# Half fills of two banks for the scores of the second layer's first pass, and a new order of steps

## The chip, the cores and the metric

The kernel runs on one core of a Trainium2 chip. The metric is the device time of one execution in microseconds (us). Times of single instructions come from one profiled execution.

## What is computed

Two transformer blocks on x of 8 images (batch entries) of 512 tokens of 256 numbers. The first block has linear and windowed attention and a gated feed; the second, which the change touches, is:

```python
x1, x2 = jnp.split(x, 2, axis=-1)                 # rotation of queries and keys
attn = jnp.einsum('bqhd,bkhd->bhqk', Q, K) * scale     # 16 heads of 16 numbers
attn = jnp.where(causal, attn, NEG_INF)
attn = jax.nn.softmax(attn, axis=-1)
out = jnp.einsum('bhqk,bkhd->bqhd', attn, V).reshape(B, S, dim)
x = x + ga * (out @ w_proj + b_proj)
h = silu(tlin(h, w1)) * tlin(h, w2)               # 256 -> 1024
h = gelu(tlin(h, h1)); h = gelu(tlin(h, h2))      # 1024 -> 1024, twice
x = x + gb * tlin(h, w3)
```

## The kernel before

The kernel is a list of steps, `ORDER`, written out as text. An entry `1:max.0.2.1` is layer 1 (the second), step `max`, image 0, group of heads 2, fill 1. Every engine walks the whole list and runs its own part of each step, so each engine works strictly in the list's order and waits on semaphores for the others.

PSUM has 8 banks. They are dealt out as named rooms: `wide` is banks 0 to 3, `low` banks 0 and 1, `high` banks 2 and 3, `acc` bank 4, `misc` bank 5, `f0` and `f1` banks 6 and 7. Each room has a semaphore for filled and one for freed, counted by `fills_of`, which also finds for each fill who used its banks last. `slot_of` names the room of a step of the second layer.

The attention of an image goes over four groups of four heads. Scores are computed twice. For the row maxima, steps `max` with j = 0, 1, 2 (L1952) write query blocks of 128 against all keys up to them: j = 0 has 512 keys, j = 1 has 384 and 128 keys, j = 2 has 256. A product takes 32 rows of the array; the four heads of a group stand on its four strips of 32 rows and in the four banks of `wide`. VectorE masks the diagonal block of the four heads (L1686) and reduces them to maxima (L1689); after j = 2 it writes the shift columns (L1697, L1698). Step `again` turns these (L1938, and L1742 on VectorE). Then steps `att` with j = 0, 1, 2 write shift plus scores with keys on the partitions (L1964, L1968), ScalarE takes the exponential of four heads at once (L1843) into one of two buffers `probs`, GpSimd zeroes what lies above the diagonal (L1608), and TensorE multiplies with the values (`values`, L1984). ScalarE releases the room only when its result is written (L1846). Steps `tq` and `tk` bring queries and keys of a group (L1931; L1832, L1835 on ScalarE, L1736 on VectorE), `heads` and `turn` carry the result back (L1993, L2002; L1749, L1751).

The second layer's first pass overlaps the first layer's last steps: `r`, `kk` and `last` (L1120, L1130 on TensorE; the mixes L742 and L745, and L752, L755, L757 on VectorE), `out` (L1108), the flag (L597 to L600, L1152). Later passes overlap with the feed of the image before them: `up` (L2025), `h1` and `h2` (L2041). `norm` normalises (L1649), `stats` is L1640 and L1643, `proj` is L1922 with the rotation on VectorE (L1666 to L1679).

Of the kernel before, what the change touches and what calls it, by code (L numbers as in the profile page):

```python
# [1227 lines left out]
0:lv.14.2 0:lin.15.1 0:wv.14.1 0:lv.15.0 0:lh.14 0:fold.16 0:pair.16 0:v.4.1 0:tq.17 0:wv.15.0 0:win.15.1 0:turn.3.2 0:again.16 0:wt.13.0 0:wt.13.1
0:lin.16.0 0:wh.14 0:tk.17 0:stats.5 0:lv.15.1 0:lv.15.2 0:wv.15.1 0:win.16.0 0:lh.15 0:lv.16.0 0:wh.15 0:fold.17 0:lin.16.1 0:turn.3.3 0:tq.18
0:turn.3.1 0:wm.17.0 0:out.3.0 0:pair.17 0:tk.18 0:out.3.1 0:lin.17.0 0:lv.16.1 0:lv.16.2 0:wt.14.0 0:wv.16.0 0:win.16.1 0:lin.17.1 0:tq.19 0:xT.3.0  # L1230
0:wv.16.1 0:wm.18.0 0:again.17 0:fold.18 0:lv.17.0 0:tk.19 0:xg.4 0:pair.18 0:lh.16 0:lv.17.1 0:xT.3.1 0:lin.18.0 0:again.18 0:fold.19 0:win.17.0
# [955 lines left out]
```

## Time and profile before

| | us |
|---|---|
| median of 3 runs | 1977.19 |
| lowest, highest | 1975.2, 1977.64 |
| profiled execution | 1979.78 |
| its span | 1978.0 |

The span is that of the trace. Times in rows count from its start. A granted clock (PEclk) of 1.00 is TensorE at 2.4 GHz, its other level is 1.2 GHz, and a mean between is time spent at both. PE is TensorE, PEld its weight loads, DVE VectorE, ACT ScalarE, POOL GpSimd. A name with q (ACTq) is the engine's queue of semaphore instructions. A wait for several semaphores is put down to the one that came last.

### The profile page before, as it was taken

The page shows a single profiled execution, that of the slowest core. Times are in us where ns is not written, and L with a number is a line of the kernel's source. Part 1 is how long each engine was busy: PE and PEld are TensorE (multiplying, and loading weights), DVE is VectorE, ACT ScalarE, POOL GpSimd, SP SyncE. Part 2 cuts the span into 40 slices and gives each one's busy share as a digit, 9 for nine tenths or more (in the row PEclk, how much of TensorE's full clock was granted, in tenths as well). Part 3 has the DMA queues.
Part 4 walks back from the last instruction along what each step waited for, and adds up shares of the span by engine and source line. Part 5 has one row for each costly group of instructions (what it writes and reads, how often), then busy time and mean ns, then how long its engine had stood idle before and what let it go on. Part 6 is the DMA issues. An engine that isn't in the chain of part 4 may idle for free.

```text
span 1978.0 us, 39009 instructions
## 1 busy us (share of the span) xinstructions
PE 1856.4 (94%) x15449; PEld 1293.8 (65%) x15449; DVE 1375.4 (70%) x2407; ACT 907.2 (46%) x1116; POOL 510.0 (26%) x597
## 2 busy tenths in 40 slices
PE   7998999899999998887999999999999999999998
PEld 4665657565666664444677676676776776776787
DVE  5667677766776677778768678587588678587443
ACT  2656574656565653332444524524534434534431
POOL 2434353443444342121211203102204003112120
PEclk8898999999999999888999999999999999999999
DMA  6221213221321110400122122221231231221321
GB/s 184 58 46 42 59 37 73 50 58 28 86 52 26 40 39 5 171 1 17 44 81 78 54 85 62 65 87 50 75 96 30 86 93 44 86 84 43 112 83 43
DMA packets 171812, 126.26 MB, mean 64 GB/s; under 512 B 113944, under 2 KB 148720, under 8 KB 171248
## 3 DMA queue, kind: packets, MB, share of 16 engines
q1 hardware_dynamic: 170800, 123.74, 22.6%
q8 instruction: 127, 2.08, 0.4%
q14 instruction: 53, 0.43, 0.1%
q10 hardware_dynamic: 832, 0.01, 0.0%
HBM read 103.66 MB, written 20.03 MB: 63 GB/s over the span
## 4 chain that ended last, share of the span: by engine, by line
PE 77%; DVE 15%; ACT 4%; issue 3%; POOL 1%; DMA 0%; SPq 0%; DVEq 0%; POOLq 0%; ACTq 0%
PE ps L2041 24%; PE ps L2025 5%; PE ps L1078 5%; PE ps L1922 4%; PE ps L1984 3%; PE ps L983 3%; PE ps L1952 3%; PE ps L2055 2%; PE ps L1108 2%; PE ps L1041 2%; PE ps L1130 2%; PE ps L1023 2%; DVE b_maxima L1689 2%; PE ps L1968 2%; PE ps L1964 2%
## 5 line engine op out<-in xcount | busy, mean ns | idle before, releaser
L2041 PE MATMUL ps<-b_acts,b_hidden_w 128*128 128x512 f32 x2048 | 504.6, 398 | 1.1 <-POOL b_acts L1616 1.1
L2041 PEld LDWEIGHTS ps<-b_acts,b_hidden_w 128*128 128x128 f32 x2048 | 376.2, 188 | 90.9 <-issue 9.8
L452 POOL TENSOR_SCALAR_AFFINE_SELECT a_probs<-a_probs 128x512 f32<-128x512 f32 (+1 forms) x224 | 166.3, 758 | 357.4 <-ACT a_probs L863 249.1
L1608 POOL TENSOR_SCALAR_AFFINE_SELECT b_work<-b_work 128x512 f32<-128x512 f32 x128 | 83.3, 663 | 673.1 <-ACT b_work L1843 673.0
L1879 ACT ACTIVATE b_acts_exact<-ps,c_s 128x512 f32<-128x512 f32 x128 | 88.2, 689 | 297.6 <-PE ps L2041 297.4
L863 ACT ACTIVATE a_probs<-ps 128x2048 f32<-128x2048 f32 (+1 forms) x96 | 153.2, 1595 | 123.5 <-DVEq L713 86.7
L1843 ACT ACTIVATE b_work<-ps 128x2048 f32<-128x2048 f32 (+1 forms) x96 | 153.4, 1597 | 90.8 <-PE ps L1968 89.0
L1689 DVE TENSOR_REDUCE b_maxima<-ps 128x4 f32<-128x2048 f32 (+3 forms) x128 | 187.9, 1489 | 3.3
L1787 DVE CAST b_acts<-b_acts_exact 128x512 fp32r<-128x512 f32 x128 | 55.8, 436 | 164.2 <-ACT b_acts_exact L1879 163.9
L1078 PE MATMUL ps<-a_probs,c_va 128*17 128x192 f32 (+4 forms) x2048 | 136.6, 388 | 2.9 <-issue 1.5
L1686 DVE TENSOR_TENSOR ps<-ps,c_causalr 128x512 f32<-128x512 f32 x128 | 86.1, 696 | 45.2 <-PE ps L1952 43.4
L1616 POOL TENSOR_TENSOR b_acts<-b_acts_exact,b_acts 128x512 fp32r<-128x512 f32 x64 | 82.5, 1289 | 134.0 <-DVE b_acts L1780 112.8
L1952 PE MATMUL ps<-c_k_split,c_q_split 32*128 32x512 f32 (+3 forms) x1024 | 68.5, 363 | 29.6 <-DVE b_maxima L1689 13.8
L1788 DVE TENSOR_TENSOR b_acts<-b_acts_exact,b_acts 128x512 fp32r<-128x512 f32 x128 | 88.7, 693 | 4.4
L1984 PE MATMUL ps<-b_work,c_va 128*17 128x512 f32 (+3 forms) x1024 | 88.4, 451 | 2.2 <-POOL b_work L1608 1.7
L1078 PEld LDWEIGHTS ps<-a_probs,c_va 128*17 128x17 f32 x2048 | 48.0, 98 | 58.9 <-issue 40.1
L1922 PE MATMUL ps<-c_wqkv,b_work 128*128 128x512 f32 (+1 forms) x256 | 85.6, 486 | 0.0
L1871 ACT ACTIVATE b_acts_exact<-ps,c_s 128x512 f32<-128x512 f32 x64 | 44.1, 689 | 89.1 <-PE ps L2025 87.6
L1952 PEld LDWEIGHTS ps<-c_k_split,c_q_split 32*128 32x128 f32 x1024 | 42.2, 192 | 63.7 <-issue 23.9
L2025 PE MATMUL ps<-b_acts,b_w2T 128*128 128x512 f32 x256 | 77.6, 426 | 0.9 <-DVEq L1795 0.6
L457 POOL TENSOR_SCALAR_AFFINE_SELECT a_probs<-a_probs 128x1024 f32<-128x1024 f32 (+2 forms) x96 | 74.7, 794 | 4.4
L2025 PE MATMUL ps<-b_acts,b_w1T 128*128 128x512 f32 x256 | 75.6, 419 | 0.3 <-issue 0.3
(244 smaller groups left out, 3577.4 us busy)
## 6 DMA issues: line engine op xcount, KB each, us to landing
b_hidden_w<-turned_h SPq DMA_DIRECT2D x128, 512.0 KB, 3.5
a_raw_next<-in_L_ffn_h_w SPq DMA_DIRECT2D x512, 16.0 KB, 1.8
turned_h<-a_staged SPq DMA_DIRECT2D x32, 256.0 KB, 2.1
a_x<-in_L_attn_x SPq DMA_DIRECT2D x8, 512.0 KB, 4.6
x_mid<-a_x SPq DMA_DIRECT2D x16, 256.0 KB, 2.2
c_x<-x_mid SPq DMA_DIRECT2D x8, 512.0 KB, 3.9
out<-c_x SPq DMA_DIRECT2D x16, 256.0 KB, 2.5
turned_w<-a_staged SPq DMA_DIRECT2D x12, 256.0 KB, 2.4
```

The source lines that it names most:

```text
L452: return nc.gpsimd.affine_select(out=z, in_=z, compare_op=ALU.is_ge, fill=0.0, base=0, pattern=[[0, blocks_n], [1, cols]], channel_multipl ...
L863: nc.scalar.activation(pb, here[:, :, o:o + w], ACT.Square, bias=1.0, scale=0.5).then_inc(att_ready, 1)
L1078: ins = nc.tensor.matmul(here[R * i:R * i + HD + 1, kb * P:kb * P + q], va[:, b % 2, kb, 4 * g + i, :], pb[:, first + i * pitch:first + i ...
L1689: ins = nc.vector.tensor_reduce(maxima[:, t, :].unsqueeze(2), room["wide"][:, :, o:o + (t + 1) * P], AX.X, ALU.max, negate=True)
L1788: nc.vector.tensor_tensor(dst[:, 1], z, dst[:, 0].bitcast(F32), ALU.subtract).then_inc(h_split, 1)
L1843: ins = nc.scalar.activation(probs[nth % 2][:, 0:4 * w].rearrange("p (h q) -> p h q", q=w), here[:, :, 0:w], ACT.Exp, scale=float(HD) ** -0.5)
L1879: nc.scalar.activation((exact_a if name == "h2" else exact_b)[:, m], here, ACT.Gelu, scale=s12[:, 2 + (name == "h2"), m:m + 1]).then_inc(g ...
L1922: ins = nc.tensor.matmul(here[:, a, 0:w], hT[:, k, t * P:(t + 1) * P], wqkv[:, k, o:o + w], start=(k == 0), stop=(k == ND - 1))
L1952: ins = nc.tensor.matmul(here[:, i, o:o + (t + 1) * P], part[rows_of(i), g % 2, t * P:(t + 1) * P], ksplit[rows_of(i), g % 2, 0:(t + 1) * ...
L1984: ins = nc.tensor.matmul(room["acc"][R * i:R * i + HD + 1, kb * P:S], va[:, kb, 4 * g + i, :], probs[nth % 2][:, i * w + o:i * w + o + S - ...
L2025: ins = nc.tensor.matmul(here, view((w1T, w2T)[j][:, i, k]), view(h2r[:, k, part]), start=(k + part == 0), stop=(k == ND - 1 and part == 1))
L2041: ins = nc.tensor.matmul(here, view(hidden_w[:, m, k]), view(src[:, k, i]), start=(k + i == 0), stop=(k == NHID - 1 and i == 1))
```

## The change

Only image 0 of the second layer is split. There each `max` becomes two steps `maxh` and each `att` two steps `atth`, with a last number 0 or 1: heads 0 and 1 of the group in room `low`, heads 2 and 3 in room `high`. Each half has its own filled and freed counts. Products, masked squares and maxima are the same in sum; each VectorE and ScalarE instruction there handles two heads instead of four, so there are twice as many. GpSimd's zeroing stays whole and runs after the second half. The order of steps is another one from image 4 of the first layer on to the last pass; most steps of the second layer's later passes keep their place within a few.

Line numbers in the changed kernel are higher: its masks are L1714, maxima L1717, score fills L1998, weight fills L2011 and L2015, the normalisation L1654.

VectorE, ahead of the passage: normalisation of the second layer's image 0 and the first layer's mixes. Before:

```order
L742 TENSOR_SCALAR a_mix<-a_xT,a_one_mu 128x512 x2
L745 SCALAR_TENSOR_TENSOR a_mix<-a_xT,a_mu,a_mix 128x512 [waits a_dve_own_result]
L745 SCALAR_TENSOR_TENSOR a_mix<-a_xT,a_mu,a_mix 128x512
L1649 TENSOR_SCALAR b_work<-c_x,b_meanvar,b_rstd 128x256 [waits b_rstd0_ready,a_sumsq_ready,a_x_plus_h_ready]
L1649 TENSOR_SCALAR b_work<-c_x,b_meanvar,b_rstd 128x256 x3
L566 RECIPROCAL a_rden<-ps 128x16 [waits m1_free,m0_full]
L568 TENSOR_TENSOR a_onat<-ps,a_rden 128x4x64 [waits a_dve_own_result]
L566 RECIPROCAL a_rden<-ps 128x16 [waits m1_free,m1_full]
L568 TENSOR_TENSOR a_onat<-ps,a_rden 128x4x64 [waits a_dve_own_result]
L755 TENSOR_SCALAR a_oT<-ps 128x512 [waits m0_full]
L757 TENSOR_TENSOR a_oT<-a_oT 128x512 [waits a_dve_own_result]
L1666 TENSOR_TENSOR b_work<-ps,c_cossin 128x512 [waits m0_full,a_staged1_placed,a_staged0_placed,high_full]
```

Now:

```order
L1654 TENSOR_SCALAR b_work<-c_x,b_meanvar,b_rstd 128x256 [waits b_rstd0_ready,a_sumsq_ready,a_x_plus_h_ready]
L1654 TENSOR_SCALAR b_work<-c_x,b_meanvar,b_rstd 128x256 x3
L742 TENSOR_SCALAR a_mix<-a_xT,a_one_mu 128x512 [waits a_xT_half_ready]
L742 TENSOR_SCALAR a_mix<-a_xT,a_one_mu 128x512
L745 SCALAR_TENSOR_TENSOR a_mix<-a_xT,a_mu,a_mix 128x512 [waits a_dve_own_result]
L745 SCALAR_TENSOR_TENSOR a_mix<-a_xT,a_mu,a_mix 128x512
L742 TENSOR_SCALAR a_mix<-a_xT,a_one_mu 128x512 x2
L745 SCALAR_TENSOR_TENSOR a_mix<-a_xT,a_mu,a_mix 128x512 [waits a_dve_own_result]
L745 SCALAR_TENSOR_TENSOR a_mix<-a_xT,a_mu,a_mix 128x512
L1645 BN_STATS b_stats<-c_x 128x6 x4
L1648 BN_AGGR b_meanvar<-b_stats 128x2 [waits b_dve_own_result]
L1648 BN_AGGR b_meanvar<-b_stats 128x2 x3
```

The mixes, and the statistics of image 2, stand behind the normalisation now, where before the mixes stood ahead of it.

VectorE, the first maxima of image 0. Before:

```order
L1686 TENSOR_TENSOR ps<-ps,c_causalr 128x4x128 [waits wide_full]
L1689 TENSOR_REDUCE b_maxima<-ps 128x4 [waits b_dve_own_result]
L1736 TENSOR_TENSOR c_q_split<-ps,c_q_split 128x512 [waits b_high_queries_turned,misc_full]
L1686 TENSOR_TENSOR ps<-ps,c_causalr 128x4x128 [waits wide_full]
L1686 TENSOR_TENSOR ps<-ps,c_causalr 128x4x128
L1689 TENSOR_REDUCE b_maxima<-ps 128x4 [waits b_dve_own_result]
L1689 TENSOR_REDUCE b_maxima<-ps 128x4
L752 SCALAR_TENSOR_TENSOR a_oT<-a_oT,a_gb 128x512 [waits a_feed_gate_ready,a_tanh_r_ready]
```

Now:

```order
L1714 TENSOR_TENSOR ps<-ps,c_causalr 128x2x128 [waits low_full]
L1717 TENSOR_REDUCE b_maxima<-ps 128x2 [waits b_dve_own_result]
L1714 TENSOR_TENSOR ps<-ps,c_causalr 128x2x128 [waits high_full]
L1717 TENSOR_REDUCE b_maxima<-ps 128x2 [waits b_dve_own_result]
L1714 TENSOR_TENSOR ps<-ps,c_causalr 128x2x128 [waits low_full]
L1714 TENSOR_TENSOR ps<-ps,c_causalr 128x2x128
L1717 TENSOR_REDUCE b_maxima<-ps 128x2 [waits b_dve_own_result]
L1717 TENSOR_REDUCE b_maxima<-ps 128x2
```

The waits for `wide` have become waits for `low` and `high` by turns, and the queries' second part (L1736) and L752 have moved out from between.

TensorE, where weight fills and score fills follow each other. Before, groups 1 and 2:

```order
L1964 MATMUL ps<-c_k_split,c_shift_rows 128x384 [waits wide_free]
L1964 MATMUL ps<-c_k_split,c_shift_rows 128x384 x3
L1968 MATMUL ps<-c_q_split,c_k_split 128x384 x8
L1964 MATMUL ps<-c_k_split,c_shift_rows 128x128 x4
L1968 MATMUL ps<-c_q_split,c_k_split 128x128 x8
L1952 MATMUL ps<-c_k_split,c_q_split 128x512 [waits misc_free,wide_free]
L1952 MATMUL ps<-c_k_split,c_q_split 128x512 x7
```

Now, groups 0 and 1:

```order
L2011 MATMUL ps<-c_k_split,c_shift_rows 128x512 [waits misc_free,low_free]
L2011 MATMUL ps<-c_k_split,c_shift_rows 128x512
L2015 MATMUL ps<-c_q_split,c_k_split 128x512 x4
L1088 MATMUL ps<-c_identr,a_sums 128x128 [waits acc0_free,m0_free]
L1088 MATMUL ps<-c_identr,a_sums 128x128 x3
L2011 MATMUL ps<-c_k_split,c_shift_rows 128x512 [waits misc_free,high_free]
L2011 MATMUL ps<-c_k_split,c_shift_rows 128x512
L2015 MATMUL ps<-c_q_split,c_k_split 128x512 x4
L1998 MATMUL ps<-c_k_split,c_q_split 128x384 [waits low_free]
L1998 MATMUL ps<-c_k_split,c_q_split 128x384 x3
```

A score fill that waited for the whole room now waits for one half, with the other half's weight fill ahead of it.

The diff; of the table one line before and one after are shown:

```diff
-0:lh.30 0:lin.31.2 1:max.0.0.0 1:tk.0.1 1:tq.0.1 0:lv.31.0 1:max.0.0.1 0:r.6.0 1:max.0.0.2 1:max.0.1.0 1:again.0.0 0:r.6.1 1:max.0.1.1 0:last.6.0
...
+0:lh.30 0:lin.31.0 0:r.6.1 1:tq.0.0 0:lin.31.1 0:kk.6.1 1:tk.0.0 0:lin.31.2 0:wh.31 1:tq.0.1 1:maxh.0.0.0.0 1:tk.0.1 1:maxh.0.0.0.1 1:maxh.0.0.1.0
...
@@ -1335,6 +1338,8 @@
     name = step[0]
     if name in ("max", "att"):
         return "wide"
+    if name in ("maxh", "atth"):
+        return ("low", "high")[step[4]]
     if name in ("hT", "xT"):
         return "low"
     if name == "proj":
@@ -1589,7 +1594,7 @@
             name, b = step[:2]
             if name == "stats":
                 power(0, b)
-            elif step == ("max", 0, 0, 2):
+            elif step == ("maxh", 0, 0, 2, 0):
                 nc.gpsimd.memset(shift_cols[:], 0.0).then_inc(shift_zero, 1)
             elif name == "ga":
 
@@ -1597,8 +1602,8 @@
                 pool.wait_ge(ga_ready, 32 * (b + 1))
                 xb = x[:, b % 3]
                 nc.gpsimd.tensor_tensor(xb, xb, ga[:, 1:2, :].broadcast_to([P, NT, D]), ALU.add).then_inc(xg_ready, 1)
-            elif name == "att":
-                g, j = step[2:]
+            elif name == "att" or name == "atth" and step[4]:
+                g, j = step[2:4]
                 nth = (b * QUADS + g) * 3 + j
                 pool.wait_ge(att_ready, nth + 1)
                 w = ATT_WIDTH[j]
@@ -1697,6 +1702,29 @@
             link(nc.vector.tensor_copy(shift_high.bitcast(F32R), maxima[:]))
             nc.vector.tensor_tensor(shift_low.bitcast(F32R), maxima[:], shift_high, ALU.subtract).then_inc(shift_ready, 1)
 
+        def half_maximum(step):
+
+            b, g, j, pair = step[1:]
+            free = arrive(step)
+            here, heads = room[slot_of(step)], slice(2 * pair, 2 * pair + 2)
+            if j + pair == 0 and g:
+                dve.wait_ge(shift_ready, b * QUADS + g)
+            for t, o in MAX_FILLS[j]:
+                square = here[:, :, o + t * P:o + (t + 1) * P]
+                ins = nc.vector.tensor_tensor(square, square, causal[:, None, :].broadcast_to([P, 2, P]), ALU.add)
+            link(ins)
+            for t, o in MAX_FILLS[j]:
+                ins = nc.vector.tensor_reduce(maxima[:, t, heads].unsqueeze(2), here[:, :, o:o + (t + 1) * P], AX.X, ALU.max, negate=True)
+            if j < 2 or pair == 0:
+                ins.then_inc(free, 1)
+                return
+            link(ins)
+            dve.sem_inc(free, 1)
+            if b + g == 0:
+                dve.wait_ge(shift_zero, 1)
+            link(nc.vector.tensor_copy(shift_high.bitcast(F32R), maxima[:]))
+            nc.vector.tensor_tensor(shift_low.bitcast(F32R), maxima[:], shift_high, ALU.subtract).then_inc(shift_ready, 1)
+
         def gated(step, gate, dst, ready):
 
             free = arrive(step)
@@ -1736,6 +1764,8 @@
                 nc.vector.tensor_tensor(qlow[:, nth % 2], room[slot_of(step)], qhigh[:, nth % 2].bitcast(F32), ALU.subtract).then_inc(free, 1)
             elif name == "max":
                 maximum(*step[1:])
+            elif name == "maxh":
+                half_maximum(step)
             elif name == "again":
                 free = arrive(step)
                 by_tile = room[slot_of(step)].rearrange("p (t q) -> p t q", q=P)
@@ -1844,6 +1874,21 @@
                 ins.then_inc(att_ready, 1)
                 act.wait_ge(att_ready, nth + 1)
                 act.sem_inc(free, 1)
+            elif name == "atth":
+                here, free = arrive(step)
+                g, j, pair = step[2:]
+                nth = (b * QUADS + g) * 3 + j
+                w = ATT_WIDTH[j]
+                if nth >= 2:
+                    act.wait_ge(pv_done, nth - 1)
+                heads = probs[nth % 2][:, 0:4 * w].rearrange("p (h q) -> p h q", q=w)[:, 2 * pair:2 * pair + 2]
+                ins = nc.scalar.activation(heads, here[:, :, 0:w], ACT.Exp, scale=float(HD) ** -0.5)
+                if pair:
+                    ins.then_inc(att_ready, 1)
+                    act.wait_ge(att_ready, nth + 1)
+                    act.sem_inc(free, 1)
+                else:
+                    ins.then_inc(free, 1)
             elif name == "values" and step[3] == 2:
                 u = fills["values", b, step[2], 0]
                 act.wait_ge(pv_done, 3 * (b * QUADS + step[2] + 1))
@@ -1940,7 +1985,8 @@
                 ins.then_inc(full_sem, 1)
 
             def max_fill(step):
-                b, g, j = step[1:]
+                b, g, j = step[1:4]
+                heads = range(4) if len(step) == 4 else range(2 * step[4], 2 * step[4] + 2)
                 here, full_sem = take(step)
                 if j == 0:
                     for name in ("tq", "tk"):
@@ -1948,24 +1994,25 @@
                         pe.wait_ge(freed[u.slot], u.free)
                 for t, o in MAX_FILLS[j]:
                     for part in (qhigh, qlow):
-                        for i in range(4):
-                            ins = nc.tensor.matmul(here[:, i, o:o + (t + 1) * P], part[rows_of(i), g % 2, t * P:(t + 1) * P],
+                        for i in heads:
+                            ins = nc.tensor.matmul(here[:, i - heads[0], o:o + (t + 1) * P], part[rows_of(i), g % 2, t * P:(t + 1) * P],
                                                    ksplit[rows_of(i), g % 2, 0:(t + 1) * P], start=(part is qhigh), stop=(part is qlow))
                 ins.then_inc(full_sem, 1)
 
             def scores(step):
-                b, g, j = step[1:]
+                b, g, j = step[1:4]
+                heads = range(4) if len(step) == 4 else range(2 * step[4], 2 * step[4] + 2)
                 here, full_sem = take(step)
                 if j == 0:
                     u = fills["again", b, g]
                     pe.wait_ge(freed[u.slot], u.free)
                 for kb, o in ATT_FILLS[j]:
-                    for i in range(4):
-                        nc.tensor.matmul(here[:, i, o:o + S - kb * P], shift_rows[rows_of(i), NT:NT + 1].broadcast_to([R, P]), shift[rows_of(i), kb * P:S],
+                    for i in heads:
+                        nc.tensor.matmul(here[:, i - heads[0], o:o + S - kb * P], shift_rows[rows_of(i), NT:NT + 1].broadcast_to([R, P]), shift[rows_of(i), kb * P:S],
                                          start=True, stop=False, skip_group_check=True)
                     for part in (qhigh, qlow):
-                        for i in range(4):
-                            ins = nc.tensor.matmul(here[:, i, o:o + S - kb * P], ksplit[rows_of(i), g % 2, kb * P:(kb + 1) * P], part[rows_of(i), g % 2, kb * P:S],
+                        for i in heads:
+                            ins = nc.tensor.matmul(here[:, i - heads[0], o:o + S - kb * P], ksplit[rows_of(i), g % 2, kb * P:(kb + 1) * P], part[rows_of(i), g % 2, kb * P:S],
                                                    start=False, stop=(part is qlow), skip_group_check=True)
                 ins.then_inc(full_sem, 1)
 
@@ -2071,9 +2118,9 @@
                     turn_nat(step)
                 elif name == "again":
                     turn_again(step)
-                elif name == "max":
+                elif name in ("max", "maxh"):
                     max_fill(step)
-                elif name == "att":
+                elif name in ("att", "atth"):
                     scores(step)
                 elif name == "values":
                     values(step)
```

## Rows read from the trace of the kernel before

**Rows 1.** The page, part 1, and part 2's granted TensorE clock in 40 slices.
```profile
PE 1856.4 (94%) x15449; PEld 1293.8 (65%) x15449; DVE 1375.4 (70%) x2407; ACT 907.2 (46%) x1116; POOL 510.0 (26%) x597
...
PEclk8898999999999999888999999999999999999999
```

**Rows 2.** Busy time of each engine by stretches; the columns are in the first line.
```profile
core 0: us, PE busy (x) PEld busy (x) DVE busy (x) ACT busy (x) POOL busy (x), PEclk, DMA share, GB/s
700.00:746.00 46.00, 41.37 (x485) 29.23 (x485) 31.30 (x57) 23.86 (x27) 21.71 (x26) 0.93 0.16 41
746.00:780.80 34.80, 30.16 (x237) 16.43 (x236) 26.82 (x51) 14.75 (x19) 9.80 (x13) 0.95 0.00 1
780.80:867.20 86.40, 66.37 (x605) 39.51 (x604) 62.77 (x100) 29.31 (x29) 12.71 (x19) 0.84 0.26 98
...
960.00:1978.00 1018.00, 994.57 (x6697) 730.77 (x6693) 696.34 (x1177) 415.03 (x473) 170.97 (x183) 0.99 0.25 72
```

**Rows 3.** Waits from 780.7 to 867.2: engine, line, waited for: us, times, longest.
```profile
DVE ps L1686 <- PE ps L1952: 14.9, 9, 4.6
...
PE ps L1964 <- ACTq L1846: 5.0, 5, 2.0
PE ps L1952 <- ACTq L1846: 4.6, 3, 2.0
```

**Rows 4.** Timeline, one turn of a score fill: TensorE, then VectorE.
```profile
820.39 0.74 PE L1952 MATMUL ps<-c_k_split,c_q_split 32*128 32x512 f32 x8 [2.02 <-ACTq L1846]
...
821.92 2.29 DVE L1689 TENSOR_REDUCE b_maxima<-ps 128x4 f32<-128x2048 f32 x1
...
824.27 0.79 PE L1952 MATMUL ps<-c_k_split,c_q_split 32*128 32x384 f32 x16 [0.98 <-DVE b_maxima L1689]
```

**Rows 5.** VectorE's groups, shapes apart, 780.7 to 867.2: count, busy, mean ns.
```profile
L1686 DVE TENSOR_TENSOR ps<-ps,c_causalr 128x512 f32<-128x512 f32 x16 | 10.8, 696 | 14.9 <-PE ps L1952 14.9
L1689 DVE TENSOR_REDUCE b_maxima<-ps 128x4 f32<-128x2048 f32 x4 | 9.2, 2292 | 0.1
L1689 DVE TENSOR_REDUCE b_maxima<-ps 128x4 f32<-128x1536 f32 x4 | 7.0, 1758 | 0.1
L1689 DVE TENSOR_REDUCE b_maxima<-ps 128x4 f32<-128x1024 f32 x4 | 4.9, 1225 | 0.1
...
L1689 DVE TENSOR_REDUCE b_maxima<-ps 128x4 f32<-128x512 f32 x4 | 2.7, 680 | 0.0
...
L1751 DVE TENSOR_TENSOR b_onat<-ps,b_rden 128x256 f32<-128x256 f32 x2 | 0.8, 424 | 0.1
...
L1640 DVE BATCH_NORM_STATS2 b_stats<-c_x 128x6 f32<-128x256 f32 x4 | 1.4, 412 | 0.0
```

**Rows 6.** Timeline of TensorE: a fill for the weights, and one dense product.
```profile
814.29 0.50 PE L1964 MATMUL ps<-c_k_split,c_shift_rows 32*128 32x512 f32 x4
814.63 0.64 PE L1968 MATMUL ps<-c_q_split,c_k_split 32*128 32x512 f32 x8
...
824.99 3.72 PE L1108 MATMUL ps<-a_wout,a_oT 128*128 128x256 f32 x16
```

**Rows 7.** The same stretch for lines L1952, L1964 and L1968 alone, in that order.
```profile
780.80:867.20 86.40, 9.30 (x120) 5.94 (x120) 0.84 0.26 98
...
780.80:867.20 86.40, 6.79 (x64) 3.42 (x64) 0.84 0.26 98
...
780.80:867.20 86.40, 8.18 (x128) 6.31 (x128) 0.84 0.26 98
```

**Rows 8.** ScalarE's smaller exponentials in the same stretch.
```profile
L1843 ACT ACTIVATE b_work<-ps 128x1024 f32<-128x1024 f32 x4 | 4.1, 1024 | 13.7 <-PE ps L1968 13.6
```

**Rows 9.** Timeline of VectorE ahead of the passage.
```profile
746.02 0.88 DVE L742 TENSOR_SCALAR a_mix<-a_xT,a_one_mu 128x512 f32<-128x512 f32 x2 [0.33 <-ACT a_xT L899]
...
751.27 3.40 DVE L1649 TENSOR_SCALAR b_work<-c_x,b_meanvar,b_rstd 128x256 f32<-128x256 f32 x4
...
761.23 0.69 DVE L1666 TENSOR_TENSOR b_work<-ps,c_cossin 128x512 f32<-128x512 f32 x1 [1.05 <-PE ps L1922]
```

More of the change, by code:

```diff
@@ L1228 @@
[L1228 to L1231, printed above, removed]
@@ new lines @@
+1:atth.0.0.0.1 1:maxh.0.1.1.0 1:maxh.0.1.1.1 0:last.6.1 1:atth.0.0.1.0 1:atth.0.0.1.1 1:maxh.0.1.2.0 0:turn.7.0 1:maxh.0.1.2.1 1:values.0.0.0
+1:atth.0.0.2.0 1:atth.0.0.2.1 1:again.0.1 1:values.0.0.1 1:tq.0.2 1:atth.0.1.0.0 0:turn.7.1 1:tk.0.2 1:atth.0.1.0.1 1:maxh.0.2.0.0 0:turn.7.2
+1:maxh.0.2.0.1 0:turn.7.3 1:values.0.0.2 1:maxh.0.2.1.0 1:maxh.0.2.1.1 1:heads.0.0 0:out.7.0 1:atth.0.1.1.0 1:atth.0.1.1.1 1:values.0.1.0
+1:atth.0.1.2.0 1:atth.0.1.2.1 1:tq.0.3 1:maxh.0.2.2.0 1:maxh.0.2.2.1 1:tk.0.3 1:maxh.0.3.0.0 1:maxh.0.3.0.1 1:values.0.1.1 1:maxh.0.3.1.0 1:again.0.2
@@ new lines @@
+1:max.2.0.1 1:tq.2.1 1:h2.0.3.1 1:h2.0.4.0 1:max.2.0.2 1:h2.0.4.1 1:tk.2.1 1:h2.0.5.0 1:heads.1.3 1:max.2.1.0 1:h2.0.5.1 1:h2.0.6.0 1:max.2.1.1
+1:h2.0.6.1 1:turn.1.1 1:h2.0.7.0 1:again.2.0 1:max.2.1.2 1:h2.0.7.1 1:out.1.0 1:att.2.0.0 1:out.1.1 1:last.0.0.0 1:att.2.0.1 1:values.2.0.0
+1:last.0.0.1 1:att.2.0.2 1:values.2.0.1 1:again.2.1 1:xT.1 1:last.0.1.0 1:split.1 1:tq.2.2 1:att.2.1.0 1:last.0.1.1 1:tk.2.2 1:up.1.0.0 1:ga.2
+1:values.2.0.2 1:max.2.2.0 1:up.1.0.1 1:up.1.1.0 1:values.2.1.0 1:heads.2.0 1:att.2.1.1 1:up.1.1.1 1:up.1.2.0 1:att.2.1.2 1:up.1.2.1 1:max.2.2.1
@@ new lines @@
+1:turn.3.1 1:h2.2.7.1 1:att.4.0.0 1:out.3.0 1:out.3.1 1:att.4.0.1 1:values.4.0.0 1:last.2.0.0 1:att.4.0.2 1:tq.4.2 1:last.2.0.1 1:xT.3 1:again.4.1
+1:last.2.1.0 1:tk.4.2 1:split.3 1:values.4.0.1 1:max.4.2.0 1:values.4.0.2 1:last.2.1.1 1:up.3.0.0 1:att.4.1.0 1:heads.4.0 1:up.3.0.1 1:up.3.1.0
+1:att.4.1.1 1:up.3.1.1 1:up.3.2.0 1:max.4.2.1 1:values.4.1.0 1:up.3.2.1 1:values.4.1.1 1:up.3.3.0 1:att.4.1.2 1:max.4.2.2 1:up.3.3.1 1:tk.4.3
+1:up.3.4.0 1:values.4.1.2 1:again.4.2 1:up.3.4.1 1:up.3.5.0 1:heads.4.1 1:att.4.2.0 1:up.3.5.1 1:up.3.6.0 1:tq.4.3 1:att.4.2.1 1:up.3.6.1 1:up.3.7.0
@@ new lines @@
+1:ga.4 1:tk.5.1 1:h2.3.4.0 1:max.5.0.2 1:heads.4.3 1:h2.3.4.1 1:h2.3.5.0 1:again.5.0 1:max.5.1.0 1:h2.3.5.1 1:h2.3.6.0 1:max.5.1.1 1:turn.4.0
+1:h2.3.6.1 1:h2.3.7.0 1:max.5.1.2 1:turn.4.1 1:h2.3.7.1 1:att.5.0.0 1:out.4.0 1:out.4.1 1:att.5.0.1 1:values.5.0.0 1:last.3.0.0 1:att.5.0.2 1:tq.5.2
+1:last.3.0.1 1:xT.4 1:again.5.1 1:last.3.1.0 1:tk.5.2 1:values.5.0.1 1:ga.5 1:split.4 1:max.5.2.0 1:values.5.0.2 1:last.3.1.1 1:up.4.0.0 1:att.5.1.0
+1:heads.5.0 1:up.4.0.1 1:up.4.1.0 1:att.5.1.1 1:up.4.1.1 1:up.4.2.0 1:max.5.2.1 1:up.4.2.1 1:values.5.1.0 1:up.4.3.0 1:values.5.1.1 1:att.5.1.2
@@ L1330 @@
+1:h2.7.7.0 1:h2.7.7.1 1:last.7.0.0 1:last.7.0.1 1:last.7.1.0 1:last.7.1.1
 """
```

190 lines of the change are left out of this document (90 added, 100 removed).

## The prediction

> **What bounds the kernel now.** I read the busy shares and the granted clock first: TensorE is busy 94% of the span, and its clock stays at full speed nearly throughout except near the start and in three slices of 49.5 us each, the 17th to the 19th, from about 790 to 940 us [rows 1]. Then the table by stretches. From 960 us on TensorE works 994.6 of 1018 us at a granted clock of 0.99: nothing can be won there by waiting less. From 780.8 to 867.2 us, which is the first pass of the second layer, it works only 66.4 of 86.4 us at 0.84, and VectorE only 62.8 of 86.4 [rows 2]. No engine is full there. The waits say why: VectorE waits 14.9 us for score fills (L1952), TensorE waits 5.0 and 4.6 us for ScalarE to release the room (L1846) [rows 3]. The timeline shows one turn: a fill of 0.74 us into all four banks, then a mask and a maximum of 2.29 us, and TensorE can write the next fill only at 824.27 [rows 4]. So the passage is bound by the one room of four banks: TensorE, VectorE and ScalarE use it by turns. What is saved there counts in full, since everything behind keeps its order and its bound.
>
> **Part 1, halves on VectorE (adds).** 16 masks of 696 ns become 32 on 256 elements; such a pass takes 424 ns [rows 5]: 13.6 against 11.1, +2.4 us. The maxima: 4 of 2292 ns become 8 of 1225 (+0.6); 4 of 1758 become 8 on 768 elements, which no row shows: between 680 and 1225, taken at 950 (+0.6); 4 of 1225 become 8 of 680 (+0.5); 4 of 680 become 8 on 256 elements, at the slope between 680 and 1225 some 410 (+0.6) [rows 5]. With 12 more handoffs on its own semaphore, estimated at 0.03 each, +5.1 us. This lies on the path, since VectorE is one of the two engines that take turns.
>
> **Part 2, halves on ScalarE.** 8 exponentials of 2048 elements and 4 of 1024 become 16 of 1024 elements (1024 ns [rows 8]) and 8 of 512. That adds about 2 us to an engine busy 29.3 of 86.4 [rows 2], and it is hidden: the first half's room is free after 1.02 instead of about 1.9 us. GpSimd masks both halves at once, after the second, and the value products behind it start no earlier than before.
>
> **Part 3, halves on TensorE.** Four heads stand on four strips of 32 rows of the array, and their products run beside each other: 8 products of 512 columns take 0.74 us [rows 4], 4 and 8 more take 0.50 and 0.64 [rows 6]. A half fill has half as many products, on two strips, with as many columns on each. No row shows two strips. Bounds: halves that run beside each other cost nothing more; at worst a half takes as long as a whole. The three lines stand for 9.3 + 6.8 + 8.2 = 24.3 us [rows 7], at full clock 24.3 x 0.84 = 20.4. I take 17 of it, near the upper end, because each strip streams the same columns and most halves have a wait between them.
>
> The Trainium skill bears on this: "TensorE: Matmul & The Clock Gate", section "Measured speedup vs the span model", gives 3.07x for four row strips of K=32. By that page a single strip takes 1/1.30 of the time of four, so a half would cost 0.77 to 1.00 of a whole, +11 to +20 us by an estimate from that figure; no run shown here tests it.
>
> **Part 4, the turns.** With two rooms VectorE works on one half while the other is refilled, so within the maxima it need not wait. It still waits where exponentials lie between two maxima, three times in each group of four heads, 12 in all: fill of a weights half (about 0.9), exponential 1.02 [rows 8], fill of a score half (about 0.7) [rows 4, 6], with handoffs 2.9 us. Its other work there covers part: 62.8 less 34.6 for masks and maxima [rows 2, 5] and 1.5 for the shift columns leaves 26.7; the new order takes out two L752, one L1736, one statistics group (1.4 [rows 5] and its small ones) and the flag, about 5.2, and brings in 0.7: 22.2, or 1.85 per turn. That leaves 1.05; I take 1.2 for products that stand between on TensorE, two of which take 3.72 us each [rows 6]. VectorE: 62.8 + 5.1 - 5.2 + 0.7 + 12 x 1.2 + 1.0 for its other waits = 78.8 us.
> TensorE by itself: 66.4 x 0.84 = 55.8 at full clock, less two products of L1130 that move ahead of the passage (half of 3.72 each, 3.7), plus 17: 69.1. The clock follows how dense it is: 90% busy in 700 to 746 went with 0.93, 87% with 0.95, 77% with 0.84 [rows 2]; at 0.94 this is 73.5. Of its 20.0 us of idle I keep 7: 80.5. The longer one decides: 80.5 against 86.4, **-5.9 us**.
>
> **Part 5, the order ahead.** VectorE's mixes of the first layer (746.02 to 751.27) stood ahead of the new layer's normalisation and now stand behind it, beside the transposes and projections for which VectorE waited until 761.23 [rows 9]. Before, 15.2 us from the first mix to the first rotation; now 3.4 + 5.3 + 2.0 + 2.1 = 12.8. But about 2.1 us of passes and 3.7 us of TensorE's products come in behind, where TensorE is already busy 30.2 of 34.8 [rows 2]. I take **-0.7**, between -2.4 and +1. The flag and one group of statistics, 3 us of VectorE, move ahead of 746, where it has 14.7 us idle but TensorE only 4.6 [rows 2]: **+1.0**, between 0 and +3. Steps of the first layer from its image 4 on and of later passes are exchanged too, a few places each; the work is the same and TensorE bound, so 0, give or take 3. DMA issues on SP hang on the same stores and are not added to.
>
> **Sum.** -5.9 - 0.7 + 1.0 = -5.6. On the profiled execution: 1979.8 (span 1978.0) to 1974.2. That execution is 2.6 above the median of 1977.2; on the median 1971.6, say **1971.5**, own range 1966 to 1976.
>
> **Rival A, the halves overlap.** If halves in a row run beside each other on the four strips, TensorE adds nothing: (55.8 - 3.7)/0.94 + 7 = 62. VectorE decides, with turns of 0.4: 63.4 + 4.8 + 1.0 = 69.2, -17.2; in all -16.9: 1960. For it: half fills of the weights stand directly behind one another in several places. Against: the second's room is often still held.
>
> **Rival B, the wait only changes its name.** TensorE's list is in order; if a 3.72 us product stands between release and refill in many turns, each costs 1.8: 63.4 + 21.6 + 1.0 = 86.0, in all 0: 1977. For it: two such products (L1108) and two half as long stand in the passage in the new order. Against: most turns have only short transposes between.
>
> **Rival C, slower: TensorE's strips.** Two of four strips for 20.4 us more, and the clock stays at 0.84 since such products leave the array sparse: (55.8 - 3.7 + 20.4)/0.84 = 86.3, with 5 of idle 91.3, +4.9; with +1.0 ahead and no gain in part 5, 1983. It decides from a clock below 0.89: 72.5/0.89 + 5 = 86.4. For it: 0.84 there today. Against: the clock is higher where the engine is denser.
>
> **How the numbers follow.** Forecast 0.42, A 0.16, B 0.20, C 0.22. A measurement can tell 0.2%, about 4 us, from no change: under 1973.2 is faster, over 1981.2 slower. Faster: two thirds of the forecast, A and some of B, 0.48; slower: C, 0.23; the rest, 0.29, within. The range must take in A and C but for their outer parts: 1960 to 1984.
>
> **What would show it.** In the changed profile VectorE's waits on score fills in the passage should fall from 14.9 to near 10 or less, TensorE's time on the three lines rise from 24.3 to about 41, its clock there to 0.9 or more, and the time from the first mask of a maximum to the next normalisation from 86.4 to about 80. From 960 on the length should stay 1018. I am wrong in part 3 if the three lines stay near 24, in part 4 if VectorE waits as long as before under other names, in part 5 if the stretches ahead of the passage or the last 1018 us change by over 3.

## The result, and the profile after

The changed kernel took 1967.2 us in the median (1963.8 to 1969.5, 5 runs) against 1977.3 (1975.2 to 1982.0, 5 runs) for the kernel before beside it: 0.9944 of it, 95% interval 0.9929 to 0.9958, or about 10 to 11 us less. The prediction said 1971.5 (own range 1966 to 1976). The profiled execution has a span of 1965.4 against 1978.0.

The page after, part 1, and the granted clock in 40 slices; they answer to [rows 1]:

```profile
PE 1864.2 (95%) x15449; PEld 1303.5 (66%) x15449; DVE 1373.5 (70%) x2439; ACT 907.0 (46%) x1128; POOL 509.2 (26%) x597
...
PEclk8898999999999998898999999999999999999999
```

Busy time by stretches. The columns and the first three cuts are those of [rows 2] (the passage is 777.6 to 858.9); the last begins some us ahead of the place that stood at 960 before. Below them the passage for L1998, L2011 and L2015 alone, which were L1952, L1964 and L1968 [rows 7]:

```profile
700.00:743.40 43.40, 40.88 (x485) 27.86 (x481) 33.42 (x70) 23.51 (x27) 21.97 (x25) 0.96 0.23 56
743.40:777.60 34.20, 30.71 (x228) 18.44 (x221) 28.55 (x56) 15.03 (x21) 9.83 (x13) 0.95 0.02 5
777.60:858.90 81.30, 75.32 (x588) 47.12 (x592) 61.32 (x120) 28.77 (x38) 11.20 (x18) 0.85 0.27 103
...
945.00:1965.40 1020.40, 997.38 (x6718) 733.48 (x6718) 698.53 (x1175) 416.03 (x475) 171.76 (x183) 0.99 0.25 72
...
777.60:858.90 81.30, 18.21 (x124) 11.90 (x124) 0.85 0.27 103
...
777.60:858.90 81.30, 11.35 (x64) 5.57 (x64) 0.85 0.27 103
...
777.60:858.90 81.30, 13.33 (x128) 10.05 (x128) 0.85 0.27 103
```

VectorE's groups in the passage, and then the waits there of VectorE and TensorE (columns as in [rows 5] and [rows 3]):

```profile
L1714 DVE TENSOR_TENSOR ps<-ps,c_causalr 128x256 f32<-128x256 f32 x32 | 12.9, 425 | 4.4 <-PE ps L1998 4.2
L1717 DVE TENSOR_REDUCE b_maxima<-ps 128x2 f32<-128x1024 f32 x8 | 9.8, 1224 | 0.3
L1717 DVE TENSOR_REDUCE b_maxima<-ps 128x2 f32<-128x768 f32 x8 | 7.7, 958 | 0.3
L1717 DVE TENSOR_REDUCE b_maxima<-ps 128x2 f32<-128x512 f32 x8 | 5.5, 692 | 0.3
L1717 DVE TENSOR_REDUCE b_maxima<-ps 128x2 f32<-128x256 f32 x8 | 3.3, 414 | 0.0
```

```profile
DVE ps L1714 <- PE ps L1998: 4.2, 6, 1.5
DVE c_q_split L1764 <- ACT c_q_split L1862: 4.1, 3, 2.4
...
PE ps L2011 <- ACT b_work L1885: 1.0, 1, 1.0
...
PE ps L1998 <- ACTq L1889: 0.7, 1, 0.7
PE ps L1998 <- ACT b_work L1885: 0.5, 2, 0.3
```

What to see: the passage fell from 86.4 to 81.3 us. VectorE's waits for score fills fell from 14.9 to 4.2 us, and TensorE's waits for ScalarE to release a room from 5.0 us (fills for the weights) and 4.6 (score fills) to 1.0 for L2011 and 1.2 for L1998. TensorE now works 75.3 of 81.3 us instead of 66.4 of 86.4. The rows of the three lines add up to 18.2 + 11.4 + 13.3 = 42.9 (24.3 before), but they overlap each other and the rest: in [rows 6] the second row begins 0.34 us after the first, which lasts 0.50. Counted once (intervals of TensorE's timeline joined, good to half a us), the three lines take 36.2 us (20.8 before) and all its other products 42.7 (47.0 before). But the passage is less than half of the change. In the timelines of VectorE, with the first mask of a maximum and the next normalisation as cuts:

| us, of the profiled executions | before | after | change |
|---|---|---|---|
| start to first mask | 780.8 | 777.6 | -3.2 |
| passage, to the next normalisation | 86.4 | 81.3 | -5.1 |
| from there to the end | 1110.8 | 1106.5 | -4.3 |

Forecast were +0.3, -5.9 and 0. So the experiments had to ask three things: do the halves gain, does the order gain, and are the first and last rows of this table real.

### The profile page after: what moved, and what is told of

It is laid out like the page before. It is cut to its first block, busy times and chain, and to the rows that moved or that the text cites. A ratio compares the mean times of both kernels' runs of the same rounds, so it can differ in the third digit from the quotient of the medians.

```text
span 1965.4 us, 39074 instructions
## 1 busy us (share of the span) xinstructions
PE 1864.2 (95%) x15449; PEld 1303.5 (66%) x15449; DVE 1373.5 (70%) x2439; ACT 907.0 (46%) x1128; POOL 509.2 (26%) x597
## 4 chain that ended last, share of the span: by engine, by line
PE 82%; DVE 12%; ACT 3%; issue 2%; SPq 0%; POOL 0%; DMA 0%; DVEq 0%; POOLq 0%; ACTq 0%
PE ps L2088 24%; PE ps L2072 5%; PE ps L1078 5%; PE ps L1967 4%; PE ps L2031 3%; PE ps L2102 3%; PE ps L1998 3%; PE ps L1108 3%; PE ps L1130 3%; PE ps L983 3%; PE ps L1041 2%; PE ps L1023 2%; PE ps L2015 2%; PE ps L2011 2%; PE ps L1003 2%
## 5 line engine op out<-in xcount | busy, mean ns | idle before, releaser
L452 POOL TENSOR_SCALAR_AFFINE_SELECT a_probs<-a_probs 128x512 f32<-128x512 f32 (+1 forms) x224 | 167.2, 762 | 361.0 <-ACT a_probs L863 255.9
L1694 DVE TENSOR_REDUCE b_maxima<-ps 128x4 f32<-128x2048 f32 (+1 forms) x112 | 164.4, 1488 | 2.9
L1873 ACT ACTIVATE b_work<-ps 128x2048 f32<-128x2048 f32 (+1 forms) x84 | 134.2, 1597 | 59.9 <-PE ps L2015 59.7
L1998 PE MATMUL ps<-c_k_split,c_q_split 32*128 32x512 f32 (+3 forms) x1024 | 76.6, 360 | 21.7 <-ACTq L1876 9.6
L1691 DVE TENSOR_TENSOR ps<-ps,c_causalr 128x512 f32<-128x512 f32 x112 | 75.3, 695 | 27.8 <-PE ps L1998 26.1
L1818 DVE TENSOR_TENSOR b_acts<-b_acts_exact,b_acts 128x512 fp32r<-128x512 f32 x128 | 88.6, 693 | 4.4
L1998 PEld LDWEIGHTS ps<-c_k_split,c_q_split 32*128 32x128 f32 x1024 | 47.6, 189 | 57.6 <-issue 26.8
L1916 ACT ACTIVATE b_acts_exact<-ps,c_s 128x512 f32<-128x512 f32 x64 | 44.0, 688 | 79.8 <-PE ps L2072 77.2
```

Of the source, the lines that this page charges most:

```text
L452: return nc.gpsimd.affine_select(out=z, in_=z, compare_op=ALU.is_ge, fill=0.0, base=0, pattern=[[0, blocks_n], [1, cols]], channel_multipl ...
L1694: ins = nc.vector.tensor_reduce(maxima[:, t, :].unsqueeze(2), room["wide"][:, :, o:o + (t + 1) * P], AX.X, ALU.max, negate=True)
L1818: nc.vector.tensor_tensor(dst[:, 1], z, dst[:, 0].bitcast(F32), ALU.subtract).then_inc(h_split, 1)
L1873: ins = nc.scalar.activation(probs[nth % 2][:, 0:4 * w].rearrange("p (h q) -> p h q", q=w), here[:, :, 0:w], ACT.Exp, scale=float(HD) ** -0.5)
L1998: ins = nc.tensor.matmul(here[:, i - heads[0], o:o + (t + 1) * P], part[rows_of(i), g % 2, t * P:(t + 1) * P], ksplit[rows_of(i), g % 2, 0 ...
```

## Experiments

Each kernel is the changed or the old one with another order string, but for e7 and e8. "Ratio" is to the kernel before on the same chip, with its 95% interval. All cuts are start times of the same two VectorE instructions as above.

| kernel | fills | order | first mask | passage | rest | ratio |
|---|---|---|---|---|---|---|
| before | whole | old | 780.8 | 86.4 | 1110.8 | |
| e1_order_alone | whole, 2nd place | new | 778.1 | 91.9 | 1107.3 | 0.9995 (0.9984-1.0006) |
| e5_order_alone_first | whole, 1st place | new | 774.7 | 85.4 | 1106.4 | 0.9945 (0.9927-0.9963) |
| e9_order_again | as e5 | new | 774.9 | 88.6 | 1107.1 | 0.9962 (0.9949-0.9975) |
| e2_halves_alone | halves | old | 780.1 | 84.4 | 1107.4 | 0.9989 (0.9979-1.0) |
| after | halves | new | 777.6 | 81.3 | 1106.5 | 0.9944 (0.9929-0.9958) |
| e10_changed_again | halves | new | 777.3 | 81.7 | 1107.1 | 0.9927 (0.9914-0.9941) |
| e3_new_then_old_tail | halves | old from 999 us | 777.1 | 83.0 | 1108.7 | 0.9945 (0.9933-0.9958) |
| e4_old_head_new_rest | halves | old to 700 us | 786.3 | 81.3 | 1106.0 | 0.9952 (0.9939-0.9964) |
| e11_new_head_only | whole | new to 700 us | 778.5 | 84.3 | 1108.3 | 0.998 (0.9966-0.9993) |
| e6_max_halves_only | maxima halved, weights whole, 2nd place | new | 777.8 | 96.4 | 1108.7 | 1.0015 (1.0004-1.0027) |
| e12_max_halves_first | the same, 1st place | new | 777.2 | 93.1 | 1108.4 | 1.0002 (0.9989-1.0015) |

e7 and e8 ran once each, in 1963.3 and 1965.5 us, and have no ratio; their passages are given below.

e4's execution began 5.4 us late in the first layer (its first divided output, L568, at 96.1 us against 90.7), so its 786.3 stands for 780.9. Smaller differences of this kind are in the other executions too: at 276 us, where all orders are still alike, they stand between 1.0 us ahead of the kernel before (e5) and 1.5 us behind it (e10 and e11).

### The order without the halves: e1, e5

The new order with whole fills, each put where the second (e1) or the first (e5) of its two half steps stood. They differ in the place of eleven of the 24 whole fills; in the other 13 the two half steps stand directly behind one another. One such place, as the order string has it (`max` is a fill for the maxima, `again` the transpose of the shifts, `att` a fill for the weights):

```
before: 1:max.0.0.2 1:max.0.1.0 1:again.0.0 0:r.6.1 1:max.0.1.1
e1:     1:max.0.0.2 0:lv.31.2 1:again.0.0 1:max.0.1.0 0:last.6.0 0:lh.31 1:att.0.0.0 1:max.0.1.1
e5:     1:max.0.0.2 0:lv.31.1 1:max.0.1.0 0:lv.31.2 1:again.0.0 0:last.6.0 1:att.0.0.0 0:lh.31 1:max.0.1.1
```

> The kernel before with the changed kernel's order, but every score fill whole (each pair of half steps merged at the place of its second half); nothing is left out. Theory (the gain has two parts that add: 5.1 us in the passage by the halves, 7.5 us ahead of it and behind it by the order): the passage from the first mask of a maximum to the next normalisation stays near 86, the first mask comes 3 us earlier than before, and the whole takes about 1970 us, 7 below before. Rival 1 (the order was searched for halves and is worth nothing without them): 1977 or more, the passage 86 or longer. Rival 2 (all is the order, the halves add nothing): 1967, the passage near 81.

> Once more the changed order with whole fills, as e1_order_alone, but each pair of half steps merged at the place of its first half; nothing is left out. e1 took 91.9 us in the passage. Theory (the changed order needs the second room, wherever a whole fill is put in it): passage 89 to 93, in all within 0.2% of before. Rival (the 91.9 came from merging at the later place, so that each fill stood behind work that has to wait): passage 86 or less, in all 1973 or less.

e1: nothing gained, the passage 5.5 us longer than before, as its first rival said. I had nearly concluded that the order is worth nothing without halves. e5 refutes it: -11 us with whole fills only, and the passage 85.4. The theory for e5 failed and its rival held; run again as e9, the same program gained 7.5 us with a passage of 88.6. VectorE's last maximum and TensorE's timeline at that place, e1, then e5:

```profile
787.51 1.22 DVE L1689 TENSOR_REDUCE b_maxima<-ps 128x4 f32<-128x1024 f32 x1
...
789.43 0.77 PE L1938 MATMUL ps<-c_identr,b_shift_cols 128*128 128x512 f32 x1 [2.15 <-DVE b_shift_cols L1698]
...
790.12 1.22 PE L1952 MATMUL ps<-c_k_split,c_q_split 32*128 32x512 f32 x8
```

```profile
784.49 1.22 DVE L1689 TENSOR_REDUCE b_maxima<-ps 128x4 f32<-128x1024 f32 x1
...
785.83 1.23 PE L1952 MATMUL ps<-c_k_split,c_q_split 32*128 32x512 f32 x8 [0.28 <-DVEq L1694]
...
787.54 0.50 PE L1938 MATMUL ps<-c_identr,b_shift_cols 128*128 128x512 f32 x1
```

In e1 the transpose of the shift columns (L1938) stands ahead of the next group's fill (L1952) and waits 2.15 us for VectorE. VectorE's last maximum ends at 788.7, which leaves the room empty; the fill behind the transpose starts only at 790.1, 1.4 us later. In e5 the fill goes first and starts 0.1 us after the maximum's end (785.7). From there to its next mask VectorE takes 2.7 us in e1 and 1.4 in e5. So one neighbour exchanged in the list costs 1.3 us here. The passages differ by 3.3 us (e9) to 6.5 (e5); what the ten other places cost no run shows one by one, and e1's granted clock in the passage was 0.80, e9's 0.81, e5's 0.88.

### The halves without the order: e2

```
-1:att.0.0.0
+1:atth.0.0.0.0 1:atth.0.0.0.1
```

> The changed kernel's half fills in the order of before, each whole step replaced in place by its two halves; nothing is left out. Theory (the halves give 5 us in the passage by themselves, TensorE's three lines cost 43 instead of 24 us there too): passage 81 to 82, 1972. Rival 1 (with two halves directly behind one another in the list and nothing between, the second waits as the whole fill did, and TensorE pays 16 us more): passage 90 or more, 1981 or more. Rival 2 (halves directly in a row overlap on TensorE and cost little there): three lines under 33 us, passage under 78, 1969.

Measured 0.9989 (interval 0 to 4 us), about 2 us; passage 84.4. Neither the theory nor a rival was met. The rows of TensorE's three lines add up to 13.6 + 10.5 + 12.4 = 36.4 us here, not 43 (counted once 29.5, not 36.2): halves directly behind one another run partly beside each other, and wholly where both rooms are free. First after, where something stands between two halves, then e2, where nothing does:

```profile
793.20 0.50 PE L2011 MATMUL ps<-c_k_split,c_shift_rows 32*128 32x512 f32 x2
...
793.54 0.63 PE L2015 MATMUL ps<-c_q_split,c_k_split 32*128 32x512 f32 x4
```

```profile
813.96 0.52 PE L2011 MATMUL ps<-c_k_split,c_shift_rows 32*128 32x512 f32 x4
...
814.29 0.65 PE L2015 MATMUL ps<-c_q_split,c_k_split 32*128 32x512 f32 x8
```

0.50 and 0.63 us for half as many products as in [rows 6], where the whole took 0.50 and 0.64: a lone half costs a whole. And 0.52 and 0.65 for both halves in a row. VectorE still waited 9.3 us for score fills in e2. That the old order leaves too little between the fills is my reading; no run shows it. In the old order whole fills took 86.4 us in the passage before and 84.3 in e11, so the halves alone gave 0 to 2 us there.

### Do the halves count in the new order: e9, e10

e5 at 0.9945 and after at 0.9944 were timed apart, with 3 us between the medians of the kernel before, so they had to be run on one chip.

> The kernel of e5_order_alone_first once more (whole fills, changed order), beside the changed kernel on the same chip, since the two were timed at 0.9945 and 0.9944 of before in different calls, while their traces differ by 4.1 us in the passage (85.4 against 81.3). Theory (the halves shorten the passage by 4 us in this order and that reaches the end): this one 3 to 4 us above e10. Rival (what the halves win is given back elsewhere, and the gain is the order's): the two within 1.5 us.

> The changed kernel itself, on the same chip as e9_order_again. Theory: 0.9925 to 0.994 of before and 3 to 4 us below e9; passage 81 to 82. Rival: within 1.5 us of e9.

1973.8 (1972.3 to 1974.2) against 1967.1 (1965.9 to 1968.2): 6.8 us between the medians, more than the 3 to 4 of the theory, and the runs don't overlap. The passage took 85.4 and 88.6 us in the two traces with whole fills, 81.3 and 81.7 with halves. So halves are worth 4 to 7 us in this order. That e5 showed none of it goes with its clock: of the eleven executions of the program with whole fills (e5, e9) the four with a granted clock of 0.977 to 0.978 took 1966.1 to 1968.4 us, the seven with 0.972 to 0.975 took 1971.7 to 1975.7; the ten of the changed kernel, at 0.972 to 0.979, took 1963.8 to 1969.5. By the medians of these eleven and ten, 1972.3 and 1967.1, the halves are worth 5.2 us. On the chip of e9 and e10 the whole change was worth 14 us (0.9927), and 7.5 of them (0.9962) are the order's.

### Where the order gains: e3, e4, e11

e3 takes the old order from image 1's first output on, e4 up to some 700 us, e11 is the kernel before with the new order up to there.

> The changed kernel, but from the first output of image 1 of the second layer on (about 999 us) the order of before. Theory (the part of the gain behind that place, 2.3 us in the traces, is the order there): 1969.5. Rival (the order there is worth nothing, the 2.3 us are what the earlier part brought): 1967.

> The changed kernel, but up to some 700 us (the fold of index 28 in the first layer) the order of before. Theory (2.2 us of the 3.15 us that the first mask comes earlier are the order of that stretch, as the hidden product of the last image shows in the traces, 636.8 against 634.6): 1969.4, the first mask of a maximum near 780. Rival (that lead would be taken up again by the waits behind it): 1967, first mask near 777.6.

> The kernel before (whole fills) with the changed order up to some 700 us (the fold of index 28 in the first layer) and its own order from there on. Traces with the old order up to there had the first mask of a maximum at 780.1 to 780.9, those with the new one at 774.2 to 778.1. Theory (the gain ahead of the passage comes from that stretch alone): first mask at 775 to 778, passage 86, in all 3 to 5 us below before. Rival (it needs the steps exchanged behind 700 us too, the mixes behind the normalisation): first mask near 780, in all within 1.5 us of before.

e11 gained 4 us by itself (0.998, interval 1 to 7 us), as its theory said, with the first mask at 778.5, just outside its 775 to 778. Since whole executions come late or early by 1 to 2 us, I count from L670 of image 3, the second step of the first layer's normalisation on VectorE, ahead of which all orders are alike. From there the first mask comes after 504.6 to 505.1 us in the three traces with the old head (before, e2, e4) and after 499.1 to 503.0 in the eleven others; before took 504.9, e11 501.2. That settles the place: the exchanges of the first layer up to 700 us. About half of it is there by the last image's L670, which comes after 360.9 to 361.0 us with the old head and 358.1 to 359.3 with the new. Inside them I have no cause; TensorE is busy 97.0 instead of 96.2 of the 100 us up to 700. The medians of e3 and e4 were 1969.1 and 1970.5 us, near their theories (1969.5 and 1969.4), but the difference of their ratios to the changed kernel's two, 0.9944 and 0.9927, is too small to price either part by time.

The same program also reaches the first mask at different times, with the clock. TensorE's row from 735 to 760 us, of after and then of e10, which is the same kernel:

```profile
735.00:760.00 25.00, 20.96 (x200) 12.38 (x203) 20.01 (x41) 9.69 (x14) 11.67 (x15) 0.86 0.01 4
```

```profile
735.00:760.00 25.00, 19.93 (x240) 12.15 (x236) 22.48 (x47) 10.37 (x15) 13.63 (x15) 1.00 0.04 12
```

And VectorE's normalisation and first mask, again after and then e10:

```profile
741.43 1.38 DVE L1654 TENSOR_SCALAR b_work<-c_x,b_meanvar,b_rstd 128x256 f32<-128x256 f32 x4
...
777.63 0.42 DVE L1714 TENSOR_TENSOR ps<-ps,c_causalr 128x256 f32<-128x256 f32 x1
```

```profile
743.04 1.76 DVE L1654 TENSOR_SCALAR b_work<-c_x,b_meanvar,b_rstd 128x256 f32<-128x256 f32 x4
...
777.29 0.42 DVE L1714 TENSOR_TENSOR ps<-ps,c_causalr 128x256 f32<-128x256 f32 x1
```

36.2 us between them at 0.86, 34.2 at 1.00: the clock is worth 2.0 us here. e3, e6 and e12 have 36.2 too, at 0.86; e5, e7, e8 and e9 have 34.2, at 1.00. What the clock cost the kernel before in this stretch, where it had 0.80, no run shows.

The tail is worth little: e3 is at 0.9945 without it. The 4.3 us behind the passage are mostly the profiled execution of before: e2 and e11 have its very order there and took 1107.4 and 1108.3, the new order 1106.0 to 1107.6 in every trace but those of e6 and e12. 1 to 2 us may be the order's.

### What limits the passage now: e7, e8

e7, in `project_out` and `feed`:

```diff
-                for k in range(2 * ND):
+                kept_k = ND if b == B - 1 else 2 * ND
+                for k in range(kept_k):
...
+            kept_k = 1 if name == "last" and b == B - 2 else ND
...
-                for k in range(ND):
+                for k in range(kept_k):
```

e8, for image 7 of the first layer:

```diff
-                statistics(1, x[:, b % XR], (2 * i, 2 * i + 1))
+                if b < B - 1:
+                    statistics(1, x[:, b % XR], (2 * i, 2 * i + 1))
...
-                    for k in range(ND):
+                    for k in range(ND if b < B - 1 else 0):
```

> The changed kernel with less work on TensorE in the passage: the first layer's last output product of image 7 (L1108) and the last product of image 6 (L1130) sum over half of their terms, 8.6 and 5.2 us fall to about half, some 6.9 us less. Theory (TensorE, busy 75.3 of 81.3 us, sets the length): passage 75 to 76. Rival (VectorE, busy 61.3 of 81.3, and the turns set it): passage 80 or more.

> The changed kernel with less work on VectorE in the passage: for image 7 of the first layer the statistics of its second norm (2.0 us) and the first step of its mix (L742, 2.2 us) are left out, 4.2 us less. Theory (TensorE sets the length): passage shorter by 0 to 1.5, 80 to 81.3. Rival (VectorE and its turns set it): shorter by 3.5 to 4.2, 77 to 78.

```profile
774.20:854.00 79.80, 73.10 (x568) 44.14 (x568) 60.93 (x119) 28.89 (x38) 11.80 (x18) 0.81 0.27 105
```

```profile
774.70:856.40 81.70, 75.10 (x588) 47.12 (x592) 57.15 (x107) 28.79 (x38) 11.27 (x18) 0.85 0.28 102
```

e7, the first row: 79.8, 1.5 shorter, where 5 to 6 were expected. e8, the second: 81.7, no shorter although VectorE works 4 us less. In this one trace VectorE's own work doesn't set the length, as the theory for e8 had it. TensorE's work hardly does either. The two lines lost 5.4 us rather than 6.9 (L1108 8.6 to 5.2, L1130 5.2 to 3.2), and TensorE's busy time only 2.2, of which 0.7 became waiting; the passage's granted clock was 0.81 where it was 0.85. Whether the lower clock came of the missing products is not shown: each of the two executions is single, and one and the same program (e5, e9) had 0.88 and 0.81 in the passage. The spread of the passage among equal orders (81.3 to 81.7 for the changed kernel's and 83.0 in e3, 85.4 and 88.6 in e5 and e9) is as large as the 1.5 us. So "TensorE sets the length" is not shown, and the theory for e7 (75 to 76) failed.

### Halves of one kind alone: e6, e12

```
-1:atth.0.0.1.0 1:atth.0.0.1.1
+1:att.0.0.1
```

> The changed kernel with halves for the maxima only; the fills for the weights are whole again, at the place of their second half. Nothing is left out. TensorE then pays about 9 us less in the passage (18.2 for the maxima stay, 24.7 for the weights fall to 15). Theory 1 (TensorE's time decides and halves of the weights bring nothing of their own): passage 76, in all 1963. Theory 2 (a whole fill for the weights needs both rooms empty, so VectorE's turn has to end first, and the next maximum waits for the whole exponential): passage 86 to 88, in all 1973.

> The changed kernel with halves for the maxima only, as e6_max_halves_only, but each whole fill for the weights at the place of its first half. e6 took 96.4 us in the passage. Theory 1 (e6 lost by the place: an order by the second place cost 6.5 us with whole fills too): passage 82 to 87, in all 1967 to 1971. Theory 2 (a whole weights fill between half fills has to wait for both rooms, wherever it stands): passage above 90, in all 1975 or more.

Passage 96.4 and 93.1, each 4.5 us longer than with no halves at all at the same places (e1 and e9; e5 was shorter still). For e12 the second theory held; e6 was longer than either of its theories said. e12's waits:

```profile
DVE ps L1712 <- PE ps L1996: 11.7, 8, 3.1
...
PE ps L2009 <- ACTq L1874: 6.3, 5, 2.0
PE ps L1996 <- ACTq L1874: 5.3, 4, 2.0
```

A whole fill for the weights (L2009) and the half fill behind it (L1996) each wait up to 2.0 us for the whole exponential, as in [rows 3]; VectorE waits 11.7 us. TensorE's rows for the maxima add up to 17.7 us instead of 10.0 (e9), and VectorE is busy 61.6 us instead of 58.1 with its smaller passes, but the rest of VectorE's passage, 31.5 us, is no shorter than e9's 30.5; with both kinds halved it is 20.0. The granted clock was also low here, 0.73 in e6 and 0.76 in e12 against 0.81 in e9, and what of the 4.5 us is the clock's was not separated.

## The prediction, step by step

- **What bounds the passage: the one room.** Held. VectorE's waits for fills fell from 14.9 to 4.2 (I said near 10 or less), and halves gain 4 to 7 us, where 5.9 was forecast for the passage.
- **Part 1, VectorE.** 12.9 + 9.8 + 7.7 + 5.5 + 3.3 = 39.2 us against 34.6: +4.6 of the 5.1. The two sizes without a row came out at 958 and 414 ns (taken 950 and 410).
- **Part 2.** Held for the exponentials: 20.4 us instead of 19.1, and no wait on them above 1.0 us. But VectorE's wait for ScalarE's copies of the queries grew from 1.6 to 4.1 us, which the forecast didn't have.
- **Part 3, TensorE.** The rows of the three lines grew by 18.6 us. Counted once they grew by 15.4 (20.8 to 36.2), about 13.3 at full clock (36.2 x 0.85 - 20.8 x 0.84), where 17 was taken; the sum 24.3 [rows 7] counts overlaps twice. And I wrote that most halves have a wait between them, but 13 of the 24 pairs stand directly behind one another in the list. The estimate by the Trainium skill, "TensorE: Matmul & The Clock Gate", section "Measured speedup vs the span model", was 0.77 to 1.00 of a whole for a half; the rows show 1.0 (0.50 and 0.63 us), its upper end, and show besides that two halves in a row cost one whole. So rival A's mechanism exists, in some places; e2 has more of it (29.5 us counted once).
- **The clock.** This step failed. I put 0.94 for a denser TensorE; it is 93% busy and has 0.85. Over the traces the busy share doesn't tell the clock of this passage: 69% busy with 0.88 (e5), 72% with 0.81 (e9), 92% with 0.81 (e7). Rival C's condition, a clock below 0.89, was met, and it was not slower: TensorE's work was smaller than its 72.5 and my 69.1 as well, 75.3 x 0.85 = 64.0 at full clock. Most of that is the 13.3 instead of 17 above, and 1.8 us more of overlap between the three lines and the rest; the products that moved away took off 4.3 us against 3.7. The two errors nearly cancel: the clock adds 69.1/0.85 - 69.1/0.94 = 7.8 us and the smaller work takes 6.0 off, so 75.3 instead of 73.5, with 6.0 of idle 81.3, forecast 80.5. That the passage came out so near is in part luck.
- **Part 4.** VectorE side 78.8, really 61.3 busy and 20.0 waiting. The waits on fills are less than 12 x 1.2, but new ones came: 4.1 us for ScalarE's copies of the queries, 2.2 for the product of L1108. Rival B happened in part.
- **Part 5, the order.** Failed. -0.7 + 1.0 + 0 was forecast; in the profiled executions the first mask came 3.2 us earlier and the part behind the passage was 4.3 us shorter, and over 3 was my sign of being wrong here. The order is worth 4 us up to 700 us alone (e11) and 7 to 11 in all with whole fills at their first places (e9 and e5), but 1 at their second (e1). I costed the edits that I could name, the mixes, the flag and the statistics, and put the many exchanges of one or two places at 0, give or take 3, since "the work is the same and TensorE bound". In a list that four engines run in order, that says nothing of the waits: e1 and e5 have the same work and differ by 10 us (by 7 where e5 was run again as e9). Which exchanges up to 700 us gain, and by what wait, stays open.

So the forecast was right in its direction and in the halves' term, and too small by what it denied the order. That 1967.2 lies inside the range of 1966 to 1976 is partly luck too: the change was 10 us at the first timing and 14 when run again (e10, 0.9927), against 6 forecast.
